# A graph network on one core: more edge positions fetched by one-hot matmuls in layers 2 and 3, and a node network whose last chunk is halved

## The reference

```python
m = jax.nn.relu(x[src] + ea) + EPS
logits = m * t
mx = jax.ops.segment_max(logits, dst, num_segments=N)
e = jnp.exp(logits - mx[dst])
denom = jax.ops.segment_sum(e, dst, num_segments=N)
alpha = e / denom[dst]
agg = jax.ops.segment_sum(m * alpha, dst, num_segments=N)
h = agg + x
h = h @ W1 + b1
h = jax.nn.relu(_ln(h, lg, lb))
return h @ W2 + b2
```

## Time and profile before

| | |
|---|---|
| median of 3 runs | 11834.85 us (11805.13 to 11844.25) |
| profiled execution, its own time | 11722.95 us |
| its span | 11721.2 us |
| mean granted TensorE clock | 0.692 |
| busy share PE, DVE, ACT, POOL | 50%, 56%, 28%, 56% |
| full windows in layer 0 | 166 to 2480 us |
| full windows in layers 1, 2 and 3 | 2686 to 9490 us, with three node networks between them |
| second stage | from about 9700 us |

### The profile page before, as it was taken

The page is one execution under the profiler, slowest core; times in us unless marked ns, Lnnn a source line. Parts: engine busy times, 40 slices in busy tenths (PEclk is TensorE's granted clock), DMA queues, the critical chain, the costliest instruction groups (busy, mean ns, idle before and its releaser), DMA issues. The chain is left out here.

```text
span 11721.2 us, 107715 instructions
## 1 busy us (share of the span) xinstructions
PE 5825.3 (50%) x31762; PEld 4080.8 (35%) x31762; DVE 6542.5 (56%) x8027; ACT 3318.9 (28%) x4928; POOL 6519.4 (56%) x6157
## 2 busy tenths in 40 slices
PE   2333333343444444534444444444444447888887
PEld 2222222232333333433333333333333334444444
DVE  5666666663444444534444445444444457988887
ACT  2333323332333333423333333333333332111110
POOL 5555555435555555455555554555555546888887
PEclk6656666566666666666666666666666668999999
DMA  5434344333333333333333333333333335555555
GB/s 157 135 129 139 132 134 139 124 114 101 118 118 118 118 118 118 103 103 119 118 118 119 118 118 103 100 118 119 118 118 119 119 106 99 97 95 99 96 97 87
DMA packets 839891, 1354.58 MB, mean 116 GB/s; under 512 B 499870, under 2 KB 555900, under 8 KB 838154
## 3 DMA queue, kind: packets, MB, share of 16 engines
q1 hardware_dynamic: 523256, 1135.94, 27.8%
q0 software_dynamic: 312640, 214.30, 12.7%
q10 hardware_dynamic: 3916, 3.40, 0.1%
HBM read 806.66 MB, written 546.46 MB: 115 GB/s over the span
## 5 line engine op out<-in xcount | busy, mean ns | idle before, releaser
L821 POOL DMA_INDIRECT xg<-h_tab,idx x4656 | 4461.3, 958 | 4294.0 <-DVE idx L1150 2821.9
L912 PE MATMUL turn<-hb,hot 125*128 125x192 bf16 x12480 | 1867.4, 293 | 2931.1 <-issue 2858.7
L912 PEld LDWEIGHTS turn<-hb,hot 125*128 125x128 fp8e4 x12480 | 1294.5, 113 | 3496.9 <-issue 3460.8
L1150 DVE COPY idx<-idx_full 128x24 int32 x208 | 36.7, 177 | 3415.5 <-ACT zl L1030 3395.9
L928 PE MATMUL turn<-ident,sums 128*128 128x128 f32 x5184 | 1077.0, 374 | 1485.7 <-ACT st_all L1045 948.3
L1513 POOL DMA_INDIRECT acc<-vm,tgt x1026 | 1601.1, 1561 | 340.1 <-issue 292.0
L928 PEld LDWEIGHTS turn<-ident,sums 128*128 128x128 f32 x5184 | 876.9, 222 | 1632.1 <-ACT st_all L1045 1051.0
L1061 ACT ACTIVATE hx<-turn 128x384 bf16<-128x384 f32 x156 | 76.4, 490 | 3505.5 <-PE turn L912 3450.9
L1045 ACT ACTIVATE st_all<-turn 128x512 f32<-128x512 f32 (+1 forms) x1344 | 751.1, 577 | 810.0 <-remote 403.0
L1157 DVE TENSOR_TENSOR_SCAN rx<-rp,carry,zl 128x1536 f32<-128x1536 bf16 (+1 forms) x224 | 740.0, 3304 | 323.4 <-ACT zl L1030 309.0
L1586 PE MATMUL zl<-spreadz,lo_hot 128*128 128x512 f32 x1620 | 778.1, 618 | 95.2 <-DVE spreadz L1762 95.2
(11 more groups left out here) (277 smaller groups left out, 7414.8 us busy)
## 6 DMA issues: line engine op xcount, KB each, us to landing
sums<-st_all SPq DMA_DIRECT2D x208, 1536.0 KB
hot<-hot_tab SPq DMA_DIRECT2D x312, 625.0 KB
ea<-feat SPq DMA_DIRECT2D x158, 768.0 KB
srcB<-src_flat SPq DMA_DIRECT2D x108, 768.0 KB
rp<-run_pen SPq DMA_DIRECT2D x210, 384.2 KB
xg<-h_tab,idx POOLq DMA_INDIRECT x4656
hot_tab<-hot SPq DMA_DIRECT2D x104, 625.0 KB
run_head<-zeros SPq DMA_DIRECT2D x216, 192.0 KB
```

The lines of the kernel that those rows point to most:

```text
L821: g_.indirect_dma_start(xg[b][:, k, h, :], None, h_tab[:, :], bass.IndirectOffsetOnAxis(ap=idx[b][:, h, k:k + 1] if small is None else idx ...
L912: ins = pe.matmul(picked[:, :, n % 2, :], hot[n][0:PN, t_, :], hb[0:PN, t_, :, :], start=t_ == 0, stop=t_ == NT - 1, skip_group_check=True)
```

## The change

A third pair of each full window is picked in layers 2 and 3, and a fourth in layer 3. The table for the third is made in layer 1, that for the fourth in layer 2. The node network gets a chunk table: nine chunks of four tiles and two of two tiles, in place of ten of four. All counts of semaphores follow.

```diff
+NODE_SIZES = [MT] * (MC - 1) + [MT // 2] * 2
+NCH = len(NODE_SIZES)
+NODE_AT = [sum(NODE_SIZES[0:k]) for k in range(NCH + 1)]
+NODE_CUTS = [slice(NODE_AT[k], NODE_AT[k + 1]) for k in range(NCH)]
+CHUNK_OF = [k for k in range(NCH) for _ in range(NODE_SIZES[k])]
...
-HOT = [0, 2, 2, 2]
-MADE_IN = [0, 0]
+HOT = [0, 2, 3, 4]
+MADE_IN = [0, 0, 1, 2]
...
                         for t_ in range(NT):
-                            if t_ % MT == 0 and t_ // MT > AHEAD:
-                                g_.wait_ge(x_ok, MC * l + t_ // MT - AHEAD)
+                            if t_ in NODE_AT and CHUNK_OF[t_] > AHEAD:
+                                g_.wait_ge(x_ok, NCH * l + CHUNK_OF[t_] - AHEAD)
...
-                        for k in range(MC + 1):
-                            if k < MC:
+                        for k in range(NCH + 1):
+                            if k < NCH:
                                 pe.wait_ge(hin_ok, base + k + 1)
-                                for j in range(MT):
+                                for j in range(NODE_SIZES[k]):
...
-                        for k in range(MC + 3):
-                            if k < MC:
+                        for k in range(NCH + 3):
+                            if k < NCH:
```

More of the change, by code:

```diff
@@ L561, in gnn @@
                 sem(n) for n in ("prow_ps", "pold_in", "pexp_ok", "patch_v", "patched"))
-            dn_in = [sem(f"dn_in{i}") for i in range(MC)]
+            dn_in = [sem(f"dn_in{i}") for i in range(NCH)]
             hin_ok, hinT_ps, hinT_sb, y_ps, ysum_ok, yroot_ok, y_ok, yT_ps, zT_sb, o_ps = (
@@ L792, in layer @@
                             load((l + 1) * LW + b, b, b, False)
-                        for k in range(MC):
-                            sp.wait_ge(h_ok, MC * l + k + 1)
+                        for k in range(NCH):
+                            sp.wait_ge(h_ok, NCH * l + k + 1)
                             store_nodes(k)
@@ L959, in layer @@
                         pe.wait_ge(patched, 32 * (l + 1))
-                        base = MC * l
-                        for k in range(MC + 1):
-                            if k < MC:
+                        base = NCH * l
+                        for k in range(NCH + 1):
+                            if k < NCH:
                                 pe.wait_ge(hin_ok, base + k + 1)
-                                for j in range(MT):
+                                for j in range(NODE_SIZES[k]):
                                     dest = ps[4][0:D, j * P:(j + 1) * P]
-                                    pe.matmul(dest, h_cur[:, k * MT + j, :], ident[:, :], start=True, stop=False)
+                                    pe.matmul(dest, h_cur[:, NODE_AT[k] + j, :], ident[:, :], start=True, stop=False)
                                     ins = pe.matmul(dest, hin[:, k % 2, j, :], ident[:, :], start=False, stop=True)
@@ L970, in layer @@
                                 pe.wait_ge(y_ok, base + k)
-                                for j in range(MT):
+                                for j in range(NODE_SIZES[k - 1]):
                                     ins = pe.transpose(ps[3][:, j * P:(j + 1) * P], y[:, j, :], ident[:, :])
                                 ins.then_inc(yT_ps, 1)
-                            if k < MC:
+                            if k < NCH:
                                 pe.wait_ge(hinT_sb, base + k + 1)
-                                for j in range(MT):
+                                for j in range(NODE_SIZES[k]):
                                     ins = pe.matmul(ps[6 + k % 2][:, j * P:(j + 1) * P],
@@ L1102, in layer @@
                                     a.wait_ge(o_ps, base + k - 1)
-                                a.activation(zT[:, :], ps[3][:, :], ACT.Relu, scale=lncur[:, 0:1], bias=lncur[:, 1:2]
+                                cols = NODE_SIZES[k - 1] * P
+                                a.activation(zT[:, 0:cols], ps[3][:, 0:cols], ACT.Relu, scale=lncur[:, 0:1], bias=lncur[:, 1:2]
                                              ).then_inc(zT_sb, 1)
-                            if k < MC:
+                            if k < NCH:
                                 a.wait_ge(y_ps, base + k + 1)
-                                for j in range(MT):
+                                for j in range(NODE_SIZES[k]):
                                     ins = a.activation(sqjunk[:, j, :], ps[6 + k % 2][:, j * P:(j + 1) * P], ACT.Square,
@@ L1111, in layer @@
                                 a.wait_ge(ysum_ok, base + k + 1)
-                                a.activation(yroot[:, k % 2, :], yroot[:, k % 2, :], ACT.Sqrt, scale=1.0 / D2, bias=ln_eps[:, 0:1]
+                                root = yroot[:, k % 2, 0:NODE_SIZES[k]]
+                                a.activation(root, root, ACT.Sqrt, scale=1.0 / D2, bias=ln_eps[:, 0:1]
                                              ).then_inc(yroot_ok, 1)
-                            if 1 < k < MC + 2:
+                            if 1 < k < NCH + 2:
                                 a.wait_ge(x_ok, base + k - 1)
-                                for j in range(MT):
-                                    ins = a.activation(sqjunk[:, j, 0:D], x_acc[:, (k - 2) * MT + j, :], ACT.Square,
+                                for j in range(NODE_SIZES[k - 2]):
+                                    ins = a.activation(sqjunk[:, j, 0:D], x_acc[:, NODE_AT[k - 2] + j, :], ACT.Square,
                                                        accum_out=xroot[:, k % 2, j:j + 1])
@@ L1217, in _ @@
                     v.memset(hinT[D:D + 1, :], 1.0)
-                    PER_LAYER = [9 + MC * 4 + (4 if SPLIT[l] else 0) for l in range(L)]
+                    PER_LAYER = [9 + NCH * 4 + (4 if SPLIT[l] else 0) for l in range(L)]
                     layer_links = [Chain(v, node_step, sum(PER_LAYER[0:l])) for l in range(L)]
@@ L1349, in _ @@
                                 v.tensor_tensor(h_cur[:, cs, :], h_cur[:, cs, :],
-                                                ncur[:, 1:2, :].broadcast_to([P, MT, D]), ALU.add).then_inc(ha_ok, 1)
+                                                ncur[:, 1:2, :].broadcast_to([P, n, D]), ALU.add).then_inc(ha_ok, 1)
                         for n, (bank, ts_) in enumerate(SPLIT_ROOMS if SPLIT[l] else []):
```

64 lines of the change are left out of this document (34 added, 30 removed).

## The result

The changed kernel takes 12237.2 us (median of 4 runs, 12227.7 to 12240.9), the kernel before beside it 11830.1 us: ratio 1.0348, 95% interval 1.0336 to 1.036. It is slower by 407 us; 12285 had been predicted. The profiled execution took 511 us more of span than that of before (12232.5 against 11721.2).

A forecast was written before the change was run, and what follows sets the result against it. The prediction took a chain to bound each window, closed by PE's picks, which crawl until the gathers stop. Picks 426, layer starts 30 and node network -6 sum to 450 us: 12173 us profiled, 12285 us median, range 12060 to 12680.

The forecast's parts named there:

- The picks: Layers 2 and 3: extra pick matmuls land behind the gathers, +2.7 and +5.5 us a window, 426 us in all.
- The clock: PE's matmuls behind the gathers start at half clock, then go mostly at full, as in an undisturbed run of 80.
- The bounds of 333 and 801 us: Limits for the picks' cost: all extra matmuls at full clock 333 us, all at half clock 801 us.
- What goes with a pick: Small matmuls, a second `hx` round and 156 more table loads on SP per execution, all covered: 0.
- rival C: Table loads miss the picks' start, so 80 more matmuls follow the gathers in layer 3: +340 us, 12630 us; chance 0.04.
- The making: 104 more tables of 5.49 us on DVE, 571 us, hidden in DVE's idle time: 0.
- rival D: The table making on DVE shows in full: +571 us, 12860 us; chance 0.04.
- Layer starts and node network: More matmuls and first table loads at the starts of layers 2 and 3, +30 us; halved node network chunks, -6 us.
- The 112 us: Added to go from the profiled execution, 11722.95 us, to the median of the runs, 11834.85 us.
- A: PE issues the extra matmuls during the gathers, so each pick saves 1.26 us: -197 us, 11640 us; chance 0.12.
- B: The extra matmuls run at half clock throughout: +801 us, 12660 us; with its neighbours, chance 0.10.
- E: No change: the saved gathers and the leftover matmuls cancel, 11835 us; chance 0.04.

The follow-up runs named there:

- e5: The kernel before with the second pick's 40 matmuls done twice in layers 1 to 3, all 22 gathers kept; 12375.1 us, ratio 1.0567 (chip 8).
- e1: The changed kernel with the third and fourth picks doing only one of their 40 matmuls, all loads and tables kept; 11825.4 us, ratio 0.9966 (chip 10).
- e3: The changed kernel with the old two picks and two tables, so only the node network's halves remain; 11853.5 us, ratio 0.9994 (chip 10).
- e2: The kernel before with the third and fourth tables also made in layers 1 and 2 but used by nobody; 11900.8 us, ratio 1.0031 (chip 10).
- e12: The changed kernel unaltered, run again on chip 15 against the kernel before; 12152.6 us, ratio 1.0371.
- e10: The kernel before with nothing picked, no table made and 24 gathers everywhere; 9063.6 us, ratio 1.0329 (chip 7).
- e11: The changed kernel with one pick in layers 1 to 3, tables made only in layer 0, `keep` ahead of the copy; 8974.6 us, ratio 1.0226 to before.
- e4: The kernel before with one pick a window in layers 1 to 3 and one table made in layer 0; 11743.9 us, ratio 0.9885 (chip 10).
- e6: The kernel before with 12 gathers a window in place of 22 in layers 1 to 3; 9751.4 us in a single run (chip 8).
- e9: The kernel before with each gather of layers 1 to 3 fetching 64 rows instead of 128; 8612.7 us in a single run (chip 7).

## Why the prediction was right

**The picks** were +426 us, 140 and 286. Measured between the two profiled executions, the 51 periods grew by 135 in layer 2 and 287 in layer 3, the whole layers by 129 and 287. The steps inside hold too: 21 and 20 gathers, 46 to 48 fast matmuls (49 before), 10 and 13 slow ones, 62 and 101 left (58 and 99 predicted). PE is freed 32.9 and 31.5 us behind the logits, against 34.1 with 22 gathers (e5): 1.26 us a gather. e1 takes the matmuls out and the loss is gone; e5 adds them without touching the gathers and costs 4.25 us for 40. Three chips agree. Two things qualify this. The prediction let the time at which the picks start set the 49; by e1 it is a count of some 60 matmuls beside the gathers. It made no difference, since the picks started nearly as early as before. And the closeness of 422 to 426 is partly luck, because it hangs on the profile of before. Against e3 on chip 10, whose windows take 42.4 us and not 41.8, the same 51 periods of the changed kernel grow by 111 and 254 us, 365 in all.

**The clock** did what the undisturbed run of the earlier trace rows did, half for 5 us and then full. The bounds of 333 and 801 us were not needed.

**What goes with a pick** was costed at 0. That is right to within some tenths of a microsecond. Of the loads I said "2 us to spare". In truth the first pick of layer 3 starts 0.8 us late (6.7 against 5.9 us), and e1 shows 22.8 us from issue to pick where I had 19.5. The wait of rival C is there, but too small to move matmuls behind the gathers. I can't say from the runs whether the loads share the engines with the gathers or wait in a queue.

**The making** was 0, measured +0.2 to +0.4 us a window (e2), about 30 us of 571. Line 1203 has its 208 instructions of 5.49 us, the scan behind waited 0.2 us for them once, and the gathers kept 1.26 us. So rival D did not come about here. Nor does the Trainium skill's rule on DVE and descriptors ("SBUF — State Buffer", the box on the "DVE blocks DMA" trap) apply: it speaks of 2-port modes, and the same page ("Who interferes with whom") says that `tensor_tensor`, the making's operation, has none. The gathers' steady 1.26 us agree.

**Layer starts and node network** were +30 - 6 = +24; the three gaps between layers grew by 30.5 us. That is near, but not for the reason given: the gap in front of layer 1, whose picks didn't change, grew by 10.7 us, those in front of layers 2 and 3 by 7.6 and 12.1. From the last chunks' first instruction to the end of DVE's part (predicted 14.0 us, 15.5 before):

```profile
2650.52 0.94 DVE L1334 RECIPROCAL node_room<-st_all 128x128 f32<-128x128 f32 x1
...
2655.31 0.94 DVE L1334 RECIPROCAL node_room<-st_all 128x128 f32<-128x128 f32 x1
...
2665.12 0.29 DVE L1360 TENSOR_TENSOR h_cur<-h_cur,ncur 128x128 f32<-128x128 f32 x1
```

14.9 us. The first half's step is 4.8 us, a full one, where I had 3.3, and the last two are 1.6 and 1.1 us where I had 2.5 and 1.5. Over the four layers the halves take 14.9, 14.9, 14.6 and 14.5 us, the chunk of before 15.5, 16.0, 15.5 and 14.7: some 3 us less in all, not 6. e3 finds no gain that can be told from none; its interval (-19 to +5 us) holds both.

**The 112 us** that I added from profile to median were wrong in kind. The change in the medians was 407 us, that in the spans 511. The sum of the terms (450) lies between. The profile of before is too fast for the runs beside the result: 11723 us is 82 us under the lowest of these, while the runs of that kernel on one chip lie within 9 to 43 us of each other. It is what chips 8 and 15 give (medians 11712 and 11718), so it may have come from another chip than the runs; the record doesn't say. The profile of the changed kernel (12234) lies within its runs. So some 100 of the 511 us are the difference between the two profiles' circumstances, not the change, and with them much of what layers 0 and 1 seem to lose. The predicted 12285 is 48 us above the measured median.

**The rivals.** A did not happen in the result or on chips 8 and 15 (e5, e12); e10 and e11 show its mechanism on chip 7. I had given it 0.12 as a way PE could behave in this program. It turned out to be what this program does on one chip of those tried; each was used once, so the chip isn't told from the state that it was in. B and E did not appear, and D only in small, in layer 0 on chip 7 (e11).

## What to carry to other kernels

Before work is moved from one engine to another, find which work ends the window and whether that work can run where the plan puts it: here a pick replaced a gather of 1.26 us by 4 us of matmuls that ran only after the gathers. An operation that is off the bound by its busy time (PE at 50%) can be the bound by when it is let run. And look at the kernel before on more than one chip before tuning a balance between two engines: here one pick less with `keep` first gained 3.3% on one chip and lost 2.3% on another.

## What the runs showed of the hardware

- In the result's run and on chips 10, 8 and 15, PE issued about one instruction in 0.7 us until 2 to 4 us after the last gather's end. This began after some 60 matmuls beside the gathers: 7.5 us after the first gather in the kernel before, 16.9 us in layer 3 of e1. In e4 its completed work reached ACT and SP only 4.2 us (median) after the gathers' end. On chip 7 neither happened, with the same gathers 1.26 us apart, and the kernel before took 8775 us instead of 11712 to 11863.
- The granted clock is no explanation: it was 0.6 in the page of e11 on chip 7 too.

```profile
PEclk6666666666666666666666666666666899999998
```

- PE was not alone. In the trace of the kernel before, from 2900 to 4700 us, 97 of SP's 773 register and wait instructions took over 0.5 us (up to 0.98), all of them while gathers ran or up to 4 us behind them. DVE, ACT and POOL had none over 0.09 us, and in e11 on chip 7 SP's longest of 860 was 0.07 us.
- The profile doesn't show PE waiting for its program to be read. It has queues for instructions (q8 and q14, 79 packets in the whole execution), and no packet of theirs in the steady windows of layers 1, 2 and 3 of the kernel before.
- What differs between the chips, and through which path the gathers hold PE, stays open. e6 shows that fewer gathers hold it for less time; whether rows or instructions count wasn't told apart, since e9 met the chip without the crawl.
